# Taking the filler products out of TensorE's queue in a two-layer vision tower

## The reference

```
h = patches @ W
h = h + delta_rule_attention(layernorm(h))          # 4 heads of 64, causal convolutions of 4 taps, output norm
h = h + top1_mixture_of_experts(layernorm(h))       # 8 experts, 256 -> 1024 -> 256, gelu
h = h + gated_delta_block(layernorm(h))             # 16 heads of 64, decay per key channel, gate, SiLU-gated feed-forward
h = h + quantized_ffn(layernorm(h))                 # 256 -> 1024 -> 256, relu, values rounded to 4/3 bits
```

## Time and profile before

| | us |
|---|---|
| median of three runs | 918.57 |
| the profiled execution | 920.19 |
| its span from first to last instruction | 918.4 |
| TensorE busy (products) | 724.3 |
| VectorE busy | 451.4 |
| GpSimd busy | 254.7 |
| ScalarE busy | 222.5 |
| mean granted TensorE clock in the span | 0.886 |

### The profile page before, as it was taken

How to read it: one execution, slowest core, us unless ns; L and a number is a source line. 1 busy time by engine, 2 the same in 40 slices (tenths; PEclk the granted TensorE clock), 3 DMA queues, 4 the chain that set the end, 5 groups by cost and what they waited for, 6 DMA issues and landing times. The chain is left out here.

```text
span 918.4 us, 20173 instructions
## 1 busy us (share of the span) xinstructions
PE 724.3 (79%) x8930; PEld 518.5 (56%) x8930; DVE 451.4 (49%) x791; ACT 222.5 (24%) x419; POOL 254.7 (28%) x251
## 2 busy tenths in 40 slices
PE   9885167983998877699788888867289788799987
PEld 5544065683987865564445445545179655555554
DVE  0677943650100103704788889877933444521230
ACT  0360122211322211230222222202433333211023
POOL 8002230003000017000788888872334100000000
PEclk9989578976999997979999999967579879999989
DMA  9000000008987821000000010000000003200000
GB/s 331 1 1 1 0 2 1 1 1 293 348 320 269 317 80 36 1 18 0 20 20 20 20 67 3 3 3 1 0 2 5 3 1 142 89 0 1 0 1 35
DMA packets 19366, 56.41 MB, mean 61 GB/s; under 512 B 4176, under 2 KB 12240, under 8 KB 14928
## 3 DMA queue, kind: packets, MB, share of 16 engines
q1 hardware_dynamic: 18512, 53.04, 15.9%
q0 software_dynamic: 768, 2.10, 0.7%
HBM read 49.60 MB, written 5.52 MB: 60 GB/s over the span
## 5 line engine op out<-in xcount | busy, mean ns | idle before, releaser
L216 PE MATMUL PS<-fill 128*128 128x256 bf16 x652 | 83.5, 282 | 3.3 <-DVE fill L1353 2.1
L216 PEld LDWEIGHTS PS<-fill 128*128 128x128 bf16 x652 | 63.8, 101 | 20.9 <-issue 5.1
L917 POOL TENSOR_TENSOR arena<-arena 128x384 f32<-128x384 f32 (+3 forms) x56 | 69.6, 1248 | 20.2 <-ACT arena L990 17.1
L1218 PE MATMUL PS<-arena 64*49 64x48 f32 (+1 forms) x3072 | 48.3, 214 | 33.8 <-DVE arena L1463 31.4
L1218 PEld LDWEIGHTS PS<-arena 64*49 64x49 f32 x3072 | 42.5, 128 | 55.9 <-DVE arena L1463 50.1
L1191 PE MATMUL PS<-Y,arena 128*128 128x392 f32 x192 | 72.5, 516 | 0.4 <-DVE beta_tok L1428 0.4
L1479 DVE COPY_PREDICATED arena<-msk,PS 128x192 f32<-128x192 int32 (+2 forms) x224 | 71.9, 442 | 0.6 <-PE PS L1218 0.6
L1139 PEld LDWEIGHTS PS<-arena 128*128 128x128 f32 x448 | 54.7, 200 | 2.4 <-issue 1.0
L1139 PE MATMUL PS<-arena 128*128 128x128 f32 x448 | 55.0, 283 | 1.2 <-DVE arena L1405 1.2
L450 PE MATMUL PS<-con,arena 32*128 32x32 f32 (+1 forms) x50 | 10.8, 363 | 54.6 <-POOL arena L353 53.8
L1150 PE MATMUL PS<-arena 128*128 128x256 f32 x224 | 52.2, 388 | 0.0
(11 more groups left out here) (209 smaller groups left out, 1305.2 us busy)
## 6 DMA issues: line engine op xcount, KB each, us to landing
arena<-in_moe_w SPq DMA_DIRECT2D x28, 1024.0 KB, 6.3
arena<-in_qka_w SPq DMA_DIRECT2D x8, 384.0 KB, 3.0
arena<-in_patches SPq DMA_DIRECT2D x3, 784.0 KB, 6.4
arena<-in_ff_w SPq DMA_DIRECT2D x1, 2048.0 KB, 8.3
arena<-in_ffn_w SPq DMA_DIRECT2D x2, 1024.0 KB, 12.7
by_expert<-arena SPq DMA_DIRECT2D x1, 1792.0 KB, 13.5
arena<-in_moe_b SPq DMA_DIRECT2D x14, 128.0 KB, 7.3
arena<-by_expert SPq DMA_DIRECT2D x14, 128.0 KB, 2.9
```

The costliest lines, as they stand in the source:

```text
L216: nc.tensor.matmul(PS[:, i, 0:2 * P], fill[:, 0:P], fill, start=True, stop=True)
L917: m = nc.gpsimd.tensor_tensor(o, s_[0], s_[1], ALU.mult)
L1218: m = nc.tensor.matmul(PS[TP * (b % 2):TP * (b % 2) + T, pb + hd, pair * 2 * ns:(pair + 1) * 2 * ns], (KB[g % 2] if l == 0 else KI[l % 2]) ...
```

## The change

All calls of `spin`, the helper itself, the tile `fill` and its memset go. `Norm.pe` loses its two parameters for the fillers. TensorE's first wait is for one signal (the memset of PSUM's last columns) instead of two. In the levels the wait on `g_kept` at levels 4 and 5, which stood ahead of a pair of fillers, goes as well; the same wait stands at the head of `lengths`, which comes next at these places. All other instructions and their order stay.

```diff
-        fill = sb("fill", P)[:, :].bitcast(BF16)
...
-        def spin(n, i):
-            for _ in range(n):
-                nc.tensor.matmul(PS[:, i, 0:2 * P], fill[:, 0:P], fill, start=True, stop=True)
...
-            def pe(self, pe, wait, spare, n_spin=16):
-                spin(n_spin, spare)
+            def pe(self, pe, wait):
                 wait(pe)
...
-                spin(10, 7)
                 for n in range(2):
                     pe.wait_ge(self.s["squared"], self.v + n + 1)
...
-                spin(30, 7)
...
-            pe.wait_ge(fill_ready, 2)
-            spin(30, 7)
+            pe.wait_ge(fill_ready, 1)
...
-            ln_a.pe(pe, wait_on(tok_kept, 4), 7, 0)
+            ln_a.pe(pe, wait_on(tok_kept, 4))
...
-            ln_b.pe(pe, wait_on(wo_kept, 4), 0)
-            ln_c.pe(pe, wait_on(res0, 2), 7, 50)
+            ln_b.pe(pe, wait_on(wo_kept, 4))
+            ln_c.pe(pe, wait_on(res0, 2))
...
-            spin(60, 7)
             pe.wait_ge(sc_step, N_ROUTE)
...
-            ln_d.pe(pe, wait_on(moe_res, BP), 0, 10)
-            rms_in.pe(pe, wait_on(Norm.s["done"], ln_d.vc + 2), 7, 50)
-            spin(40, 7)
+            ln_d.pe(pe, wait_on(moe_res, BP))
+            rms_in.pe(pe, wait_on(Norm.s["done"], ln_d.vc + 2))
...
                 for hd in range(2):
-                    if g + 1 == FT:
-                        spin(2, 0)
-                    elif between[hd] is not None:
+                    if g + 1 < FT and between[hd] is not None:
                         between[hd](g + 1)
-                    elif l >= 4:
-                        pe.wait_ge(g_kept, 6 * (g + 2))
-                        spin(2, 0)
-                    elif l == 1:
-                        spin(2, 3)
...
-            rms_ff.pe(pe, wait_on(ow_kept, 8), 0, 30)
+            rms_ff.pe(pe, wait_on(ow_kept, 8))
...
-            ln_e.pe(pe, wait_on(ff_res, 4), 7, 20)
+            ln_e.pe(pe, wait_on(ff_res, 4))
...
-            nc.vector.memset(fill, 0.0).then_inc(fill_ready, 1)
```

## The result

The changed kernel takes 923.19 us (median of 13 runs) against 918.57 for the kernel before (13 runs): ratio 1.0055, 95% interval 1.0035 to 1.0074, so 0.35 to 0.74% slower, 3.2 to 6.8 us. A second set gave 1.0045 (1.0029 to 1.006). One of the changed kernel's 13 runs took 3557.34 us and is left out of the ratio; the median of the other twelve is 923.05. The forecast was 925.5 us, with 922 to 928.5 as its own range. The profiled execution took 923.93 us, 3.7 more than that of before, where the sum for it had +8.0 (928.2).

What follows compares the result with a forecast made beforehand. No single bounding engine: TensorE-rate stretches alternate with norms and recurrences where TensorE waits. Place-by-place clock losses less blocking gains summed to +8.0 us against the profile, +6.9 against the 918.57 us median: 925.5 us, range 922 to 928.5 (66%).

Steps and rivals of the forecast that it cites:

- norm behind the delta rule: Norm after the second delta rule: idle becomes 5.6 us, L245's first half runs at low clock; +1.1 us (-0.2 to 1.3).
- the fourth norm: Fillers block L238, which starts 1.45 us sooner but runs low longer: -0.6 us; -0.7 with the norm behind it.
- the start: Token products L1035 start 1.2 us sooner but at low clock, costing 2.2: +1.0 us (+0.5 to +1.6).
- Then L1301: the clock was full there: Feed-forward products L1301 restart low after over 5 us of idle: +2.2 us (0 to 2.8), 1.1 against the median.
- The sum by that rule, +5.8: By the skill's idle limit L1301 was already low, its term nothing: +5.8 us against the median, or 924.4 us.
- the second norm: Gap ahead of L238 becomes 2.3 us: a third of 1.3 lost, less 0.2 for ten fillers; +0.3 us (-0.2 to 2).
- The third norm: Idle becomes 10.3 us, so L238 restarts low: +1.1 us, and +0.3 for L1105 behind it.
- The last norm: Idle ahead of L238 becomes 4.1 us, all eight records on the chain: +2.0 us (0 to +2.6); L1330 unchanged.
- The norm behind the fourth: L245 starts 1.4 us sooner without 90 fillers, minus 1.3 for four records at low clock: -0.1 us.
- The fillers only block: Rival, whole kernel: restarts stay fast or rise almost at once, leaving only gains: -5.7 us, or 912.9; chance 6%.
- The levels lose their clock: Rival: each of the seven groups has a low stretch, 5.6 us instead of 0.5: +12.0, or 930.6 us; chance 15%.
- Only the longest gaps pay: Rival: gaps of about 4 us and less leave the clock alone: +2.2, or 920.8 us; chance 13%.

Runs made afterwards that it cites:

- the trimmed kernel: Kernel before with fillers cut only where they end after the next product could start (17 instead of 30 at the start, others reduced or removed); 0.996, 915.14 us.
- the kernel with 108 fillers: Kernel before with 108 instead of 40 fillers ahead of L1179, nothing else changed; 0.9971 (0.9957 to 0.9985), 2.7 us faster.

## Why the prediction was right, and where not

The stages by their mean over all profiles with the fillers of that place as before and without them (in brackets how many), measured between VectorE instructions, beside the term of the sum (8 instead of 10 fillers inside a norm counts as the same). The second delta rule has no fillers; its two groups are the profiles with and without those of the last group ahead of it:

| stage | with | without | measured | predicted |
|---|---|---|---|---|
| start to first centring | 25.28 (7) | 25.93 (4) | +0.65 | +1.0 |
| first norm to first convolution | 14.41 (8) | 15.47 (4) | +1.05 | +1.2 |
| output of delta rule, second norm | 85.09 (7) | 84.56 (4) | -0.5 | +0.3 |
| third norm to ranks | 34.82 (6) | 35.81 (4) | +1.0 | +1.4 |
| fourth norm to the groups | 57.22 (6) | 56.80 (4) | -0.4 | -0.7 |
| first seven groups | 205.70 (8) | 205.55 (5) | -0.15 | +0.5 |
| last group's end | 4.00 (7) | 2.92 (4) | -1.1 | -1.0 |
| second delta rule | 130.25 (7) | 129.68 (6) | -0.6 | 0 |
| norm behind the delta rule | 44.41 (7) | 46.25 (4) | +1.8 | +1.1 |
| L1301 (30 fillers or none ahead) | 12.90 (7) | 12.67 (4) | -0.2 | +1.1 |
| last norm and L1330 | 106.86 (8) | 109.81 (4) | +2.95 | +2.0 |
| sum | | | +4.5 | +6.9 |

The measured sum is 4.5; the timed ratio 1.0055 is 5.1 and the second one 4.1. Two rows hold what is not the fillers': without the one profile of 207.61 us the groups come to +0.1, and without the two profiles whose clock stayed full in L553 (43.20 us) the norm behind the delta rule has 44.90 with fillers, a difference of 1.35. The expert stage is not in the table: it varied by 4 us with no order in it. The second delta rule's -0.6 is a difference of means in stretches that vary by 2 us, and the fourth norm's -0.4 one in stretches that vary by over 1. That 6.9 came as near to 4.5 as it did is in part luck: by this table some terms were too high, by 4.35 in all, and others too low, by 1.95. The mechanism was right: fillers buy clock behind idle gaps and cost time where they stand in front of a ready product; where both meet, as at the start and in the fourth norm, the two terms subtract. The shape of the losses was read from the right rows: one half of a norm is four records, 4 x 0.33 = 1.3, and it came out at 1.35 behind the delta rule (with 0.2 of fillers saved), 1.40 at the third norm's centring and 1.40 at the last norm's.

The step that failed is "Then L1301: the clock was full there" with +2.2 against the profile and 1.1 against the median. It rested on one execution. With the 30 fillers and 3.69 us of idle, one profile in seven kept the full clock there (11.06 us for the stretch; the others 12.75 to 13.75), and by the means taking these fillers out cost nothing (-0.2). In the pair of profiles that the forecast was made from it did cost something, 1.5 us (11.06 and 12.52), where 2.2 stood. The Trainium skill (TensorE: Matmul & The Clock Gate, "Why this matters for your kernels") tells to leave no idle between bursts beyond a limit, which these gaps pass, for the engine then goes back to half rate. I set that aside for one row; the other six profiles, with 3.68 or 3.69 us of idle, agree with it. The sum by that rule, +5.8, was nearer to the measured 4.6 than mine.

The smaller misses: the second norm lost no clock in its gap, which is 2.08 us (0.33 and 16 fillers of 0.11 make 2.1, not the 2.3 of the prediction), and kept the gain of its ten fillers, 0.17 us; the products ahead of it were a little faster too (0.35 us, in a stretch that varies by 0.9; why is open). The third norm got its 1.4 at the centring and 0.5 at L1105, but 0.7 came back at the ranks, where the clock rose sooner. The last norm lost more than 2.0: in each of the four profiles without fillers 1.40 up to the first centring and 1.29 from there to the first inversion (L272), because both halves of L238 and the start of L245 were low. The stretch behind it, with L1330, adds 0.3 by its mean but takes 29.4 to 31.0 us with the fillers and without: L1330's 24 records took 11.16 us in the changed kernel's first profile and 9.60 in its second, against 10.82 before. The norm behind the fourth gave no gain: L245 took 4.65 us for eight records instead of 2.80, more than the 1.3 that was set against its earlier start, and from the fourth norm's first centring to that norm's first inversion the profiles without fillers take 0.1 to 1.2 us longer.

"The fillers only block" had real gains (the trimmed kernel earns 3.7 of its 5.7), but the losses that it left out are there. "The levels lose their clock" happened once in thirteen profiles, and that one had the pairs. "Only the longest gaps pay" is refuted by the last norm, where a gap of 3.97 us cost 1.4 at the first half of L238 in all four profiles without fillers.

## What to carry to other kernels

A filler does two things, and they are to be counted apart, place by place: what the next real product would have started earlier, and what it then runs at. It pays most when it ends just before the next product is ready and leaves no idle: ahead of L1105, 58 fillers that left 0.2 us of idle made the kernel 3.4 us faster where 30 that left 3.3 had not kept the clock. Ahead of L1301, 30 that left 3.7 us bought nothing by the means; 60 that left 0.4 had the full clock in their profile, but no gain in the timed runs. A full clock ahead of a gap is no promise: in two of nine profiles with 30 or 34 fillers at the first norm it fell all the same, behind the next gap of 1.9 us. A step that rests on the clock in one execution needs a second profile first.

## What the runs showed of the hardware

With the same 30 fillers and 3.68 or 3.69 us of idle ahead of it, L1301 kept 2.4 GHz in one profile; in three it began at 1.2 GHz, and in three the clock fell 0.25 to 0.9 us behind its start. So a gap of that length goes either way. L1049's first bank, after 3.95 us of idle, ran nearly all at the full clock in one profile without fillers (1.61 us for 4 records) and at the low one in the other of the same kernel (2.95 us).

The thirteen profiles hold 85 gaps of 5.48 us or more that TensorE entered at the full clock, and all of them ended at 0.50. Short gaps are not safe either: behind the second norm's 2.08 us the clock stayed full in all four profiles, but behind the 1.99 us ahead of L545 it fell within 1.4 us of the restart in eleven of thirteen, and behind the 1.88 us at L1049 in two of nine with fillers.

A busy engine did not always keep its clock: behind 32 records of 16 columns, in which TensorE was busy for 3.47 of 3.80 us, it fell to 0.50 in the kernel with 108 fillers. Small products gain from the full clock as the large ones do: 32 records took 3.75 us at full clock and 7.01 at the low one with 16 columns, and 3.74 against 6.99 (changed kernel) with 8.
